# Layer norm, attention and ternary FFN on one core: masks and normalisation move to other engines, and the last token tiles get banks and buffers of their own

## The reference, cut to what matters

```python
xn = (x - mean(x)) / sqrt(var(x) + 1e-5)          # x: 2048 tokens x 256, fp32
qkv = xn @ Wqkv.T                                  # 16 heads of 128
w = softmax(q @ k.T * 128 ** -0.5)                 # per head, 2048 x 2048
attn = concat_heads(w @ v) @ Wout.T
quantize(W) = clip(round(W / (mean(abs(W)) + 1e-8)), -1, 1)
ffn = (sigmoid(xn @ quantize(w1).T) * (xn @ quantize(w2).T)) @ quantize(w3).T   # hidden width 704
out = x + attn + ffn
```

## Time and profile before

| | |
|---|---|
| time, median of 3 | 1899.84 us (1899.81 to 1901.06) |
| profiled execution | 1899.86 us, its span 1898.0 us |
| busy | PE 1855.2, DVE 1599.3, POOL 1358.2, ACT 1254.7 us |
| FFN groups 1 to 3 | begin at 57.57 us, the heads at 104.10 us |
| last result in `y` | 1894.59 + 0.88 us |

### The profile page before, as it was taken

One profiled execution on the slowest core, in us unless ns is written; L12 is line 12 of the kernel. 1 busy time (PEld: TensorE's weight loads), 2 busy tenths in 40 slices (PEclk: granted clock), 3 DMA queues, 4 the chain that ended last, 5 costly groups with the idle time before them and its releaser, 6 DMA issues.

```text
span 1898.0 us, 33380 instructions
## 1 busy us (share of the span) xinstructions
PE 1855.2 (98%) x11556; PEld 1659.1 (87%) x11556; DVE 1599.3 (84%) x2098; ACT 1254.7 (66%) x1702; POOL 1358.2 (72%) x515
## 2 busy tenths in 40 slices
PE   5979999999999999999999999999999999999998
PEld 4869888898989889898888989888898988899887
DVE  7478888888888888888888889888898988888895
ACT  4456666776667677666767666676766667676664
POOL 4438677876868787686877768687776868776675
PEclk9999999999999999999999999999999999999999
DMA  3037667676767767676776767677676767767664
GB/s 125 1 92 170 162 160 180 156 170 161 168 162 163 182 152 173 159 167 162 166 179 153 171 159 169 161 170 176 154 170 160 167 162 172 174 153 171 158 160 127
DMA packets 195912, 298.73 MB, mean 157 GB/s; under 512 B 37905, under 2 KB 57105, under 8 KB 195857
## 3 DMA queue, kind: packets, MB, share of 16 engines
q1 hardware_dynamic: 195856, 298.08, 67.1%
HBM read 12.71 MB, written 2.10 MB: 8 GB/s over the span
## 4 chain that ended last, share of the span: by engine, by line
PE 79%; POOL 6%; SPq 5%; issue 4%; DVE 3%; DMA 1%; ACT 1%; POOLq 0%; DVEq 0%; ACTq 0%
PE ps_o L398 31%; PE ps_s L389 10%; PE ps_s L390 10%; PE ps_s L391 10%; SPq L306 4%; POOL parts L1120 4%; PE ps_t L379 4%; PE ps_t L369 4%; PE ps_s L360 3%; PE ps_s L435 2%; PE ps_o L407 1%; PE ps_o L409 1%; PE ps_o L408 1%; DVE prob L969 1%; DMA raw<-prob 1%
## 5 line engine op out<-in xcount | busy, mean ns | idle before, releaser
L1120 POOL TENSOR_TENSOR parts<-raw,parts 128x2048 fp32r<-128x2048 f32 x254 | 1175.3, 4628 | 441.7 <-ACT parts L732 441.3
L744 ACT ACTIVATE prob<-ps_s,neg_max 128x1024 f32<-128x1024 f32 x512 | 567.0, 1114 | 448.6 <-DVE neg_max L963 448.6
L959 DVE TENSOR_REDUCE row_max<-ps_s 128x1 f32<-128x1024 f32 x512 | 613.1, 1213 | 113.4 <-PE ps_s L391 95.2
L969 DVE STREAM_TRANSPOSE prob<-prob 128x1024 f32<-128x1024 f32 x508 | 599.5, 1218 | 58.4 <-ACT prob L744 58.0
L732 ACT CAST parts<-raw 128x2048 fp32r<-128x2048 f32 x254 | 486.4, 1915 | 102.8 <-DMA raw<-prob 102.6
L398 PE MATMUL ps_o<-parts,v_hi 128*128 128x256 f32 x4064 | 515.6, 280 | 2.8 <-POOL v_lo L1113 2.8
L398 PEld LDWEIGHTS ps_o<-parts,v_hi 128*128 128x128 f32 x4064 | 497.9, 189 | 18.4 <-POOL v_lo L1113 5.9
L389 PE MATMUL ps_s<-k_hi,q_hi 128*128 128x512 f32 x1024 | 403.2, 394 | 11.2 <-ACT prob L744 10.3
L390 PE MATMUL ps_s<-k_lo,q_hi 128*128 128x512 f32 x1024 | 401.0, 392 | 0.0
L391 PE MATMUL ps_s<-k_hi,q_lo 128*128 128x512 f32 x1024 | 400.6, 391 | 0.0
L398 PE MATMUL ps_o<-parts,v_lo 128*128 128x256 f32 x2032 | 275.7, 278 | 0.0
(11 more groups left out here) (115 smaller groups left out, 1564.7 us busy)
## 6 DMA issues: line engine op xcount, KB each, us to landing
raw<-prob SPq DMA_DIRECT2D x2032, 128.0 KB, 2.4
v_raw<-v_turned SPq DMA_DIRECT2D x244, 64.0 KB, 2.0
w_raw<-wqkv_dram SPq DMA_DIRECT2D x32, 128.0 KB, 2.6
y<-x_dram SPq DMA_DIRECT2D x4, 512.0 KB, 4.8
wo_raw<-wqkv_dram SPq DMA_DIRECT2D x16, 128.0 KB, 2.5
wo_raw<-wo_dram SPq DMA_DIRECT2D x16, 128.0 KB, 2.3
out_dram<-y SPq DMA_DIRECT2D x8, 256.0 KB, 2.7
w_raw<-w_dram SPq DMA_DIRECT2D x2, 704.0 KB, 7.6
```

The costliest lines, as they stand in the source:

```text
L744: nc.scalar.activation(tile, logit, ACT.Exp, bias=neg_max[:, t:t + 1], scale=SCALE, accum_out=row_sum[:, t, half:half + 1]).then_inc(s_exp, 1)
L959: nc.vector.reduce_max(row_max[:, t, half:half + 1], ps_s[:, 2 * half:2 * half + 2, :].rearrange("p b n -> p (b n)"), AX_X).then_inc(s_mx, 1)
L969: nc.vector.transpose(tile, tile).then_inc(s_xp, 1)
L1120: nc.gpsimd.tensor_tensor(half_of(0, half), moved(p, half), half_of(1, half), ALU.subtract).then_inc(s_pl, 1)
```

## The change

Start. GpSimd no longer makes the three masks and `xn` of group 3. VectorE makes the masks (`mask`), and ScalarE makes `xn` of groups 1 to 3 as `rstd * y + shift`; for that `layernorm` gets one more small instruction, `shift = -mean * rstd`. `statistics(3)` comes before the first split, `layernorm(1)` between `xt_low(0)` and `xt_low(1)`, and the total of w3 is summed into `ps_o` after `keys(3)` and not in bank 3 before `transpose_x(3)`. `shift` takes its 16 columns from a filler, so that all later addresses stay.

End. The third turned quarter goes to `ps_t` and the fourth to `ps_s[0:2]`; the product of tiles 14 and 15 has bank `ps_s[2]`, its projection `ps_s[3]`, and its `o_hi` and `o_lo` lie in the query weights' buffer `w_sp[:, 0]`. Two of ScalarE's steps trade places, TensorE's steps are in another order, the pair 14, 15 is projected, added and stored ahead of 12, 13, and 12 and 13 are stored one by one.

```diff
-        ps_last = ps_t[:, 0, 0:2 * P]
+        ps_last = ps_s[:, 2, 0:2 * P]
+        ps_y_last = ps_s[:, 3, :]
+        last_o_hi, last_o_lo = [w_sp[:, 0, c].rearrange("p w d -> p (w d)") for c in range(C)]
         def last_turned(n):
-            return ps_s[:, n % 2 * 2:n % 2 * 2 + 2, :].rearrange("p b (k q) -> p (b k) q", q=2 * P)
+            banks = (ps_s[:, 0:2, :], ps_s[:, 2:4, :], ps_t[:, :, :], ps_s[:, 0:2, :])[n]
...
@@ SP @@
-            for p in range(PAIRS):
+            for p in range(PAIRS - 2):
...
+            sp.wait_ge(s_yacc_last, 2)
+            sp.dma_start(out_v[:, T - 2:T, :], y[:, T - 2:T, :]).then_inc(s_out, 16)
+            for t in (T - 4, T - 3):
+                sp.wait_ge(s_yacc, T * H + t + 1)
+                sp.dma_start(out_v[:, t, :], y[:, t, :]).then_inc(s_out, 16)
@@ TensorE, start @@
-            pe.wait_ge(s_gamma, 3)
-            totals(3, slice(2, 3))
             transpose_x(3)
...
-            pe.wait_ge(s_gamma, 6)
+            pe.wait_ge(s_gamma, 3)
             keys(3)
+            totals(3, ps_o[:, 0], slice(2, 3))
@@ TensorE, end @@
             product_step(end, 5, 1)
-            for n in (2, 3):
-                pe.wait_ge(s_llo, n - 1)
-                turn_last(n)
+            turn_last(2)
+            pe.wait_ge(s_llo, 1)
+            turn_last(3)
+            pe.wait_ge(s_llo, 2)
+            products_last(0)
             output_step(end, 5)
             product_step(end, 6, 0)
-            products_last(0)
-            product_step(end, 6, 1)
             pe.wait_ge(s_llo, 4)
             products_last(1)
+            product_step(end, 6, 1)
+            pe.wait_ge(s_olo_last, 1)
+            out_projection(ps_y_last, last_o_hi, last_o_lo, s_y_last)
             output_step(end, 6)
-            output_step(end, 7)
@@ ScalarE, start @@
+            def normalise(g):
+                act.wait_ge(s_shift, g // 2 + 1)
+                for t in range(g * TG, (g + 1) * TG):
+                    last = nc.scalar.activation(xn[:, t, :], y[:, t, :], ACT.Identity, bias=shift[:, t:t + 1],
+                                                scale=rstd[:, t:t + 1])
+                last.then_inc(s_xn_behind, 1)
             part_high(2, origin, 0)
+            normalise(1)
             xt_high(0)
             abs_sums(0, w1_raw)
             xt_high(1)
+            root(1)
             abs_sums(1, w2_raw)
             keys_high(origin, 0)
             queries_high(origin, 0, ps_v[1])
-            root(1)
+            normalise(2)
+            normalise(3)
+            keys_high(origin, 1)
+            xt_high(2)
             abs_sums(2, w3_raw)
-            keys_high(origin, 1)
-            xt_high(2)
             xt_high(3)
@@ ScalarE, last head, end @@
+                    if final and t == T - 1:
+                        last_high(0)
+                        high(h, 6, 0, True)
+                        last_high(1)
...
-            last_high(0)
-            last_high(1)
             output_high(end, 5)
             high(end, 6, 1, True)
             last_high(2)
             last_high(3)
+            act.wait_ge(s_lpv, 2)
+            nc.scalar.copy(last_o_hi, ps_last).then_inc(s_ohi_last, 1)
             output_high(end, 6)
-            act.wait_ge(s_lpv, 2)
-            act.wait_ge(s_y, count(8, end, 7))
-            nc.scalar.copy(o_hi[:], ps_last).then_inc(s_ohi, 1)
@@ VectorE @@
+            def mask(i, raw):
+                if i == 2:
+                    dve.wait_ge(s_wq, 1)
+                    dve.wait_ge(s_w3_again, 16)
+                dve.wait_ge(s_gamma, 6 if i == 2 else 3)
+                nc.vector.tensor_scalar(below_of(i, raw), raw[:], half_gamma[:, 1, i:i + 1], None, ALU.is_lt
+                                        ).then_inc(s_below, 1)
...
             for b in range(FB):
                 hidden(0, b)
+                if b == 1:
+                    mask(2, w3_raw)
                 if b == 2:
                     quantise(2, w3_raw, w3_q[:])
...
+            dve.wait_ge(s_ohi_last, 1)
+            nc.vector.tensor_tensor(last_o_lo, ps_last, last_o_hi, ALU.subtract).then_inc(s_olo_last, 1)
             output_low(end, 6)
+            dve.wait_ge(s_inv, count(8, end, 8))
+            dve.wait_ge(s_y_last, 1)
+            add_result(7, ps_y_last, s_yacc_last)
             result(end, 6)
-            dve.wait_ge(s_ohi, count(8, end, 8))
-            nc.vector.tensor_tensor(o_lo[:], ps_last, o_hi[:], ALU.subtract).then_inc(s_olo, 1)
-            result(end, 7)
@@ GpSimd @@
-            def is_below(i, raw):
...
-            for t in range(3 * TG, T):
-                last = nc.gpsimd.tensor_scalar(xn[:, t, :], y[:, t, :], mean[:, t:t + 1], rstd[:, t:t + 1],
-                                               ALU.subtract, ALU.mult)
-            is_below(0, w1_raw)
-            is_below(1, w2_raw)
-            is_below(2, w3_raw)
```

More of the change, by code:

```diff
@@ L126, in build @@
             newton = sb("newton", [P, T], where=early)
+            shift = sb("shift", [P, T], where=early)
             sig = sb("sig", [P, 2, CH], where=early)
-            sb("beside_first_values", [P, 296], where=early)
+            sb("beside_first_values", [P, 280], where=early)
             first_values = sb("first_values", [P, S], where=early)
@@ L846, in layernorm, with normalise_first @@
                 nc.vector.tensor_tensor(rstd[:, t], rstd[:, t], newton[:, t], ALU.mult).then_inc(s_ln, 1)
-            def normalise(g):
-                dve.wait_ge(s_ln, 8 * (g // 2) + 8)
-                for t in range(g * TG, (g + 1) * TG):
+                dve.wait_ge(s_ln, step + 8)
+                nc.vector.scalar_tensor_tensor(out=shift[:, t], in0=mean[:, t], scalar=-1.0, in1=rstd[:, t],
+                                               op0=ALU.mult, op1=ALU.mult).then_inc(s_shift, 1)
+            def normalise_first():
+                dve.wait_ge(s_ln, 8)
+                for t in range(TG):
                     last = nc.vector.tensor_scalar(xn[:, t, :], y[:, t, :], mean[:, t:t + 1], rstd[:, t:t + 1],
@@ L904, in _ @@
             layernorm(0)
-            normalise(0)
-            normalise(1)
+            normalise_first()
             statistics(2)
+            statistics(3)
             xt_low(0)
+            layernorm(1)
             xt_low(1)
-            statistics(3)
-            layernorm(1)
-            normalise(2)
+            thresholds(1, ps_s[:, 3, 0:2], slice(0, 2))
             keys_low(origin, 0)
+            mask(0, w1_raw)
             queries_low(origin, 0, ps_v[1])
-            thresholds(1, ps_s[:, 3, 0:2], slice(0, 2))
             values_turn(origin, 0, ps_v[0], early_turned[0])
+            quantise(0, w1_raw, w1_q[:, :, 0:FF])
             xt_low(2)
@@ L982, in inverse, with add_result @@
                 nc.vector.reciprocal(inv_denom[:, 2 * p:2 * p + 2], denom[:, 2 * p:2 * p + 2]).then_inc(s_inv, 1)
+            def add_result(p, src, added):
+                for j in range(2):
+                    t = 2 * p + j
+                    nc.vector.scalar_tensor_tensor(out=y[:, t, :], in0=src[:, j * DIM:(j + 1) * DIM],
+                                                   scalar=inv_denom[:, t:t + 1], in1=y[:, t, :],
+                                                   op0=ALU.mult, op1=ALU.add).then_inc(added, 1)
             def result(h, p):
@@ L986, in result @@
                 dve.wait_ge(s_y, count(8, h, p + 1))
-                for j in range(2):
-                    t = 2 * p + j
-                    nc.vector.scalar_tensor_tensor(out=y[:, t, :], in0=ps_y[:, j * DIM:(j + 1) * DIM],
-                                                   scalar=inv_denom[:, t:t + 1], in1=y[:, t, :],
-                                                   op0=ALU.mult, op1=ALU.add).then_inc(s_yacc, 1)
+                add_result(p, ps_y, s_yacc)
             def head(h, first, final):
```

50 lines of the change are left out of this document (24 added, 26 removed).

## The result

| | before | after |
|---|---|---|
| time, median | 1899.91 us (1899.63 to 1901.06, 6 runs) | 1888.04 us (1886.92 to 1890.0, 6 runs) |
| ratio | | 0.9937, interval 0.9926 to 0.9947 |
| block 0 of the FFN starts | 34.94 | 31.59 |
| FFN group 1 starts | 57.57 | 48.62 |
| last exponential ends | 1870.75 | 1863.37 |

The change makes the kernel 11.9 us faster; 1888.8 us was forecast. The profiled execution of after is at 1890.0 us (span 1888.2), 2 us above its median, so only stretches of it are read here, and not its total.

What follows compares the result with a forecast made beforehand. TensorE, busy 98% of the span, was taken as the bound, with gains only in its idle and slow stretches: 1899.86 - 8.2 (start) - 2.9 (end) = 1888.8 us, range 1885.5 to 1893.0.

Steps and rivals of the forecast that it cites:

- The start, 8.2 us forecast: Up to FFN group 1: earlier masks and weights bring its start from 57.57 to 49.4, gaining 8.2 us.
- Masks at 1.6 us by the `xn` row: VectorE's masks: 1.6 us each, from the 256-element `xn` row of 0.406 us, read as 1.0 ns an element.
- the rival at double rate: VectorE's masks take 0.87 us each, 0.8 us earlier at two places: 1887.2 us; chance 0.13.
- ScalarE's normalisation between 0.3 and 0.404 us: ScalarE's 256-column `xn`: at most a same-sized cast's 0.404 us, at least 0.3 start to start; `xt_high(2)` at 23.
- The replay's sum: VectorE's queue before block 0: from 15.9, inverse deviation 2.2, shift 0.2, root wait some 0.3, giving 18.3 us.
- The low end of the gain, 5.5: Start: gain of 5.5 us if ends of waits are each 1 us worse and the clock costs 1.8 us.
- Quantising with GpSimd idle 1.6 us; the 3.59 us for w2 gone: Ternary weights before and in block 0: 1.6 us each on VectorE, w2 ready at 32.0, its wait gone whole.
- Group 0 with 2.0 us of waits and group 1 at 49.4: First FFN group: 15.5 us of work plus waits of 0.8 before block 4 and 1.2 before block 5, 17.5 us.
- The rival of a low clock: Half-rate clock through the first FFN group and work ahead: 1904.3 us, chance 0.02; short fall 1890.6 to 1893.8.
- The heads slide as a whole: The 16 heads keep instructions, addresses and order, so they start and end 8 us earlier, following TensorE's arrival.
- the sign that I had named as proof against me: A last exponential not 8 us earlier although group 1 is would prove the prediction wrong.
- The end, 2.9 us forecast: Behind the last exponential: last result at 1892.4, before 1895.47, less 0.2 us for stores; gain 2.9, range 2.0 to 3.5.

Runs made afterwards that it cites:

- the rates experiment: Changed kernel with eight `tensor_scalar` of 256 and 1280 columns, constants or columns as scalars, ahead of VectorE's work; one execution, block 0 at 34.79 us, total not read.
- the kernel with GpSimd kept busy: Changed kernel, masks on VectorE, plus four GpSimd comparisons of 1024 columns whose result nobody reads; 1889.62 us, one execution.
- the kernel with GpSimd's masks: Changed kernel with the three masks back on GpSimd, all else as after; 1893.88 us, ratio 0.9964.
- the kernel with the start alone: Changed kernel with everything of the end (banks, order, stores) put back; 1892.42 us, ratio 0.9956 to before.
- the kernel with the end alone: Changed kernel with everything of the start (GpSimd's masks, VectorE's and GpSimd's `xn`) put back; 1897.02 us, ratio 0.9982 to before.

## Why the prediction was right

**The start, 8.2 us forecast.** 8.95 us in the profile, 8.3 in the timed runs. The mechanism was right, the masks' place and what they had held up, but two of its costs were wrong and cancelled by luck. Step by step:

- *Masks at 1.6 us by the `xn` row.* Wrong: 0.95 and 0.91. This is the rival at double rate, to which I had given 0.13. I set it aside on a row that is too short to show a slope, as the rates experiment shows. The Trainium skill ("VectorE: DVE Perf Modes", The perf-mode tier table) has it so, and the trace agrees. The rival's price was off too: it gave 0.8 us twice, but only the first mask lay on the path to block 0, and there ScalarE took the gain back (next point).
- *ScalarE's normalisation between 0.3 and 0.404 us.* Wrong: 0.50 from start to start (4.05 for eight). I bounded a biased, scaled activation by a plain cast. So `xt_high(2)` came at 24.36 and not 23, and VectorE, early by its mask, waited 0.72 us. The two errors nearly cancel, which is luck: block 0 at 31.59, forecast 31.9.
- *The replay's sum.* 15.9 + 2.2 + 0.2 + 0.3 is 18.6, not 18.3: the wait for the root was named and not added. Measured, it was 0.57 us, and split 1 began at 18.15, since the split before it ended at 15.57 and not 15.9. The low end of the gain, 5.5, does not add up either: 8.2 less two waits of 1 us and 1.8 for the clock is 4.4.
- *Quantising with GpSimd idle 1.6 us; the 3.59 us for w2 gone.* Right: 1.65, 1.55, no wait.
- *Group 0 with 2.0 us of waits and group 1 at 49.4.* The waits are 0.32 and 0.73 us, and group 1 starts at 48.62. The third mask was sized about right (2.06, forecast 2.3); the chain sigmoid, `hidden`, bank had half a microsecond more room at either block than I gave it. Yet group 0 is only 0.5 us shorter than forecast (17.03, not 17.5): the 0.5 us of refill that the reckoning of before had found were left out of this one.
- *Clock full from 30 to 50.* Right: 1.00 and 1.00. The rival of a low clock did not come with the one stop of 1.75 us that is left, nor with one of 2.71 in the kernel with GpSimd kept busy. The clock fell with stops of 3.16 and 3.59 us close together before and with the one of 5.25 in the kernel with GpSimd's masks.

Of the start's gain, then, 5 to 6 us hang on the masks having left GpSimd. That is more than the first mask's own 2.9 us: VectorE's queue stood behind GpSimd, its weight was slowed threefold, and the clock fell. The rest, from the normalisation's move and the new order, was not run apart.

Why does block 0 scatter by 1 us between kernels with the same start? The rows point at TensorE's first matmuls for the keys. In after the second starts at 16.30 and the third at 16.72, 0.42 us apart; in the kernel with the start alone it is 0.23, and there ScalarE's eight normalisations start at 19.32 and not 19.95. The granted clock is 1.00 in these rows, so they do not say what makes these matmuls slow.

**The heads slide as a whole.** Right up to the last head: ScalarE's exponentials are 8.79 us earlier at the start of the first head, 8.43 to 8.64 at the start of heads 2 to 15 and 8.35 at that of the last. The clock falls in the first head in both kernels, and by the same amount. The windows of after and of before across it:

```profile
100.00:125.00 25.00, 17.30 (x60) 13.01 (x60) 19.95 (x21) 12.35 (x20) 2.32 (x4) 0.86 0.42 97
125.00:150.00 25.00, 22.50 (x138) 19.47 (x137) 20.64 (x24) 18.52 (x24) 22.88 (x9) 1.00 0.76 176
```
```profile
100.00:125.00 25.00, 19.32 (x92) 15.51 (x91) 17.64 (x22) 9.87 (x17) 2.60 (x4) 0.93 0.24 55
125.00:150.00 25.00, 20.36 (x104) 16.53 (x103) 20.71 (x24) 17.93 (x25) 17.81 (x7) 0.93 0.68 157
```

Yet the last exponential is only 7.4 us earlier in this profile, though group 1 is 8.95 earlier. By its letter this is the sign that I had named as proof against me. About 1 us goes in the last head. A part of it is seen in the chain of waits there, which runs through SP's issues: they take 0.60 us, but now and then far more. After, then before:

```profile
1835.69 1.63 SPq L315
...
1859.54 1.98 SPq L315
```
```profile
1844.18 1.03 SPq L306
...
1867.01 1.71 SPq L306
```

The first long issue costs after 0.60 us more ahead of the last exponential. The second, 0.27 us more, stands in the chain that leads to the DMA of pair 6 and not to the last exponential; that DMA landed 0.27 us later behind it (2.68, before 2.41). The other profiles speak for chance in the main: from the start of group 1 to the last exponential, before and the kernel with the end alone take 1813.18 us, after 1814.75, the start alone 1815.50, and the other kernels with a changed start 1813.05 to 1814.67. That a changed start costs the heads half a microsecond in the middle (the median of all eleven with a changed start is 1813.74) is not excluded; no experiment was made on it.

**The end, 2.9 us forecast.** 24.72 us before; 22.24 after, 21.53 with the end alone. Right in kind and size: the turns are without a wait, there is 0.22 us ahead of the last projection, and 2.59 us follow the last `y` (forecast 2.7). The replay's own figure from the last exponential to the last `y` was 21.65. Most of the spread goes with the landing of pair 6's DMA, which no step of mine had as a variable: ScalarE starts on it 2.41 us behind the last exponential before, 2.68 after, 2.30 with the end alone. In the kernels with the whole end of after, ends of 21.46 to 21.84 us go with 2.15 to 2.31, and ends of 22.04 to 22.32 with 2.59 to 2.84. Of the gain 0.7 us are the banks and 0.9 or a little more ScalarE's order; the remaining 1 to 1.5, TensorE's new order and the own buffers of the last projection, were not run apart. In the profile of after 0.40 us of "issue", which nothing in the trace explains, stand ahead of the last `y`.

## What to carry to other kernels

Before an instruction's rate is read off a row, ask whether the row is long enough to tell a slope from a fixed cost: 256 columns at 0.406 us fitted both rates, and only a second width decided for the mask's form. When work leaves a slow engine that shares its path with a fast one, count three gains and not one: the work itself, the queue of the fast engine that waited for it, and the fast engine's own instructions that ran beside it. When single profiles are compared, compare first when their DMAs landed: half a microsecond there hid most of what a bank was worth. And look at how far the same mark scatters between kernels that share the stretch: block 0 moved by 1 us with no edit at all.
